# Second attention: GpSimd's sum ahead of its power, the next rows' load in slot 0, ScalarE's high half ahead of the norm

## The chip, the core and the metric

One core of a Trainium2 chip runs the whole program in one launch. The metric is the device time of one execution in microseconds. Of the kernel before three runs are given; their median is 3105.54 us.

## What is computed

Two layers, each an attention over a context and a mixture of eight experts, every one behind a layer norm and with its input added. The change lies in the second layer's attention. There x has 16 batches of 128 rows of 512 values, the context 128 further rows for each batch:

```python
q = (draft_hidden @ Wq.T).reshape(bsz, draft_len, H, HD)        # H = 16 heads of HD = 128
q = _rms_norm(q, q_norm_w).transpose(0, 2, 1, 3)
kv_in = jnp.concatenate([context_hidden, draft_hidden], axis=1) # 256 keys
k = (kv_in @ Wk.T).reshape(bsz, total_len, KVH, HD)             # KVH = 4
v = (kv_in @ Wv.T).reshape(bsz, total_len, KVH, HD).transpose(0, 2, 1, 3)
k = _rms_norm(k, k_norm_w).transpose(0, 2, 1, 3)
q = _rope(q, draft_position_ids)
k = _rope(k, full_position_ids)
scores = jnp.einsum('bhqd,bhkd->bhqk', q, k) * SCALE
probs = jax.nn.softmax(scores, axis=-1)
attn = jnp.einsum('bhqk,bhkd->bhqd', probs, v)
return attn.transpose(0, 2, 1, 3).reshape(bsz, draft_len, H * HD) @ Wo.T
```

## The kernel before

The program runs four parts in turn: first attention, first experts, second attention (`layer1_attention`), second experts. Precision close to float32 comes from splitting each operand into a high and a low float16 half; a product is three matmuls (high by high, high by low, low by high). So every value that goes into a product is made twice: ScalarE writes the high half (a copy to float16), VectorE subtracts it and writes the low half.

In the second attention a batch b has eight jobs, the projections `JOBS1` = KC, KD, Q0, VC, Q1, VD, Q2, Q3 (keys and values of context C and of x, D; four groups of four heads of queries), and four attention steps a = 0 to 3, one for each group of heads. Every engine has one queue, written by `run_pipeline` from a list of (kind, offset, stage). Time is counted in slots, eight to a batch. In each slot an engine goes through its list in the order written: a "job" stage with offset n runs job t - n, an "att" stage runs step a at slot `SCORE1[a]` + n, with `SCORE1` = 6, 8, 10, 12 (so a batch's attention runs beside the projections of the next one and the one after), an "in" stage with offset n runs in slot n for the batch after, an "end" stage n slots after the last score. The order inside a slot is the order of the list, and nothing is reordered at run time: what waits holds up all that stands behind it on its engine. The first two batches and the last two are written out, the rest is a loop.

The stages that the change and the prediction speak of, with the names of their tiles:

- SyncE's queue: `x_load` loads the next batch's x (`xt`, L1527) and context (`cx`, L1528), once the previous x is normed and the previous context split; `q_turn` (L1575) and `p_turn` (L1548) transpose by DMA the halves of the normed queries and keys and of the attention weights; `x_turn` (L1559) those of x.
- TensorE: `project` (12 matmuls of 512 columns into one of three banks `mm`), `scores` (`scb`, 12 matmuls of 256 columns), `pv` (attention output, `ovb`, 6 matmuls), `out_project` (`prb`, 12 matmuls). In even slots stand project, scores, out_project, in odd ones project, pv. `out_project(a)` stands one slot behind `pv(a)` and waits for `o_low(a)`.
- VectorE: `stats` reads a projection: four BN statistics (L1712) and the two products of the rotary embedding, `r1` and `r2` (L1717, L1720). `smax` (L1736) is the row maximum, `row_scale` (L1742, L1743) the reciprocal of the sums, `q_low` (L1731), `x_low` (L1692), `p_low` (L1750, four instructions) and `o_low` (L1758) the low halves.
- GpSimd: `scales` (L1988 to L1996) makes the RMS factors from the statistics, with a power (L1993, four values a row), and then the sum of the rotary products, `r1 + r2` (L1996, 128x512). `c_low` is the low half of the context, `tables` the sine and cosine tables.
- ScalarE: `c_high` (L1860) the high half of the context, `p_high` (L1907), `exps` (L1898) the exponentials with their row sums, `normalise` (L1878) the sum scaled by its RMS factor, in four instructions, `q_high` (L1889), `o_high` (L1914), `v_high` (L1867).

`o_high` is in the same odd slot as `exps` of two steps on, four slots behind the row maximum of its own step: in slot 3, for instance, ScalarE does the exponentials of step 2, norms Q0 and evicts the output of step 0.

Of the kernel before, what the change touches and what calls it, by code (L numbers as in the profile page):

```python
# [6 lines left out]
ALU = mybir.AluOpType  # L7
# [943 lines left out]
NN1, NV1, NA1 = len(NORM1), len(V1), 4  # L951
# [476 lines left out]
def layer1_attention(nc, I, x2_dram, x3_dram, w, wo, sincos, disp, expert_of_tile, row_of_tile, tile_oh):  # L1428


    with ExitStack() as ctx:
# [17 lines left out]
        r1 = s.sb("r1", [P, 2, 4, HD], F32)  # L1449
        r2 = s.sb("r2", [P, 2, 4, HD], F32)  # L1450
# [29 lines left out]
        rnb, rsum, rinv = (rc[:, n:n + 1] for n in range(3))  # L1480
# [25 lines left out]
        def at(k, per, b):  # L1506
            return b * per + (k + 1)

        def is0(b, k=0, below=1):

            return isinstance(b, int) and b == 0 and k < below
# [8 lines left out]
        def _(sp):  # L1520
# [40 lines left out]
            def q_turn(b, t, q):  # L1561
# [3 lines left out]
                for half, done in ((0, "qhi"), (1, "qlo")):  # L1565
# [5 lines left out]
                    if half == 0 and n >= 2 and not is0(b):  # L1571
# [2 lines left out]
                    out = kT[half][:, q, :, n, :] if n < 2 else qT[half][:, n - 2, :].rearrange("p (i t) -> p i t", t=P)  # L1574
                    sp.dma_start_transpose(out, nq[half][:, n % 2, :]).then_inc(q_turned[half][n % 2], 16)  # L1575

            run_pipeline(sp, [("in", 5, x_turn), ("job", 2, q_turn), ("att", 3, p_turn), ("end", 7, store), ("end", 2, residual), ("in", 1, x_load)],
                         NJ1, SCORE1, None, 2, HEAD1)
            sp.wait_ge(sem["out"], 16 * (B + 1))

# [259 lines left out]
        def _(act):  # L1840
# [29 lines left out]
            def normalise(b, t, q):  # L1870
                if t in v_no:
                    return
                job, n = norm_no[t], norm_no[t] % 2
                act.wait_ge(sem["rsum"], at(job, NN1, b))
                if not is0(b, job, 2):
                    act.wait_ge(sem["qlo"], at(job - 2, NN1, b))
                for i in range(4):
                    ins = act.activation(nrm[:, n, i * P:(i + 1) * P], r1[:, n, i, :], ACT.Copy,  # L1878
                                         scale=sc[:, n, 1, i:i + 1])
                ins.then_inc(sem["norm"], 1)  # L1880
# [51 lines left out]
            def r_gates(b, k, q):  # L1932
# [2 lines left out]
                act.activation(xr[:, q, DM + 1:RW], rex, ACT.Copy, scale=rinv).then_inc(sem["r_gate"], 1)  # L1935

            run_pipeline(act, [("in", 2, c_high), ("att", 2, p_high),
                               ("att", 1, exps), ("job", 1, normalise), ("job", 1, q_high),
                               ("att", 5, o_high), ("job", 1, v_high), ("in", 4, x_norm), ("in", 4, x_high),
                               ("end", 10, r_norm), ("end", 12, r_keep), ("end", 15, r_exp), ("end", 17, r_gates)],  # L1940
                         NJ1, SCORE1, None, 2, HEAD1)

# [1 line left out]
        def _(pool):  # L1944
# [33 lines left out]
            def scales(b, t, q):  # L1978
                if t in v_no:
                    return  # L1980
                job, n = norm_no[t], norm_no[t] % 2
                pool.wait_ge(sem["stat"], at(job, NN1, b))
                if not is0(b, job, 2):
                    pool.wait_ge(sem["norm"], at(job - 2, NN1, b))

                c = [sc[:, n, i, :] for i in range(2)]
                mean, spread = st[:, n, :, :, 1], st[:, n, :, :, 2]
                ch.link(pool.tensor_tensor(sq[:, n, :, :], mean, mean, ALU.mult))  # L1988
                ch.link(pool.tensor_scalar(sq[:, n, :, :], sq[:, n, :, :], HD / 2.0, None, ALU.mult))
                ch.link(pool.tensor_tensor(sq[:, n, :, :], sq[:, n, :, :], spread, ALU.add))  # L1990
                ch.link(pool.tensor_tensor(c[0], sq[:, n, :, 0], sq[:, n, :, 1], ALU.add))
                ch.link(pool.tensor_scalar(c[0], c[0], 1.0 / HD, 1e-6 * WS * WS, ALU.mult, ALU.add))
                pool.tensor_tensor(c[1], c[0], half[:, 0:4], ALU.pow).then_inc(sem["scal"], 1)  # L1993
                pool.wait_ge(sem["rot"], at(job, NN1, b))
                pool.wait_ge(sem["scal"], at(job, NN1, b))
                pool.tensor_tensor(r1[:, n, :, :], r1[:, n, :, :], r2[:, n, :, :], ALU.add).then_inc(sem["rsum"], 1)  # L1996

            def r_scale(b, k, q):
                pool.wait_ge(sem["r_stat"], b + 1)
# [366 lines left out]
```

## Time and profile before

| | |
|---|---|
| median of three runs | 3105.54 us (3100.19 to 3106.0) |
| the profiled execution, its own time | 3106.21 us |
| its span (first to last instruction) | 3104.4 us |
| mean granted TensorE clock | 0.970 |
| busy: TensorE, VectorE, ScalarE, GpSimd | 2848.2, 1829.6, 1703.5, 1741.2 us |
| second attention | about 2020 to 2812 us of the span |

The rows further down come from one profiled execution. A row of the waits says who waited for whom, in total, how often, and the longest. A row of the timeline has the start in microseconds from the span's start, the duration, the engine (SPq is SyncE's queue), the line, the operation and its output and input, and in square brackets how long the engine had idled before it and who ended that. Rows of one line are merged (x4). A matmul is pipelined: it is shown 0.38 us long, and the next begins before it ends.

### The profile page before, as it was taken

How to read it: one execution, taken by the hardware profiler on the slowest of the kernel's cores; microseconds unless marked ns; L12 is line 12 of the kernel's file. 1: busy time of each engine (PE TensorE's matmuls, PEld its weight loads, DVE VectorE, ACT ScalarE, POOL GpSimd, SP SyncE). 2: the span in 40 equal slices, each digit the busy share in tenths (PEclk: the TensorE clock that was granted, in tenths of full speed). 3: DMA queues.
4: the chain of work that ended last, by engine and by line, in shares of the span. 5: the costliest groups of instructions: out<-in, count | busy, mean ns of one | idle time of the engine just before them, and what ended most of it. 6: DMA issues, size and time to landing. Idle time of an engine off the chain costs nothing. (4 is left out here: it accounts for less than half of the span.)

```text
span 3104.4 us, 57661 instructions
## 1 busy us (share of the span) xinstructions
PE 2848.2 (92%) x16353; PEld 1637.9 (53%) x16354; DVE 1829.6 (59%) x5590; ACT 1703.5 (55%) x4562; POOL 1741.2 (56%) x2443
## 2 busy tenths in 40 slices
PE   4699999999999969999999999769999999985998
PEld 2366666666666635555555554335444444443665
DVE  4366666666666655444344344458888888863443
ACT  5578777877778732333233223346666666661332
POOL 6467777777777534554444455366666666631222
PEclk9799999999999989999999999889999999997999
DMA  6711121112111153554555456535555545657444
GB/s 241 251 42 56 51 86 48 48 55 79 58 48 55 54 200 120 161 157 125 147 159 151 137 141 186 141 80 113 122 113 123 122 112 122 123 106 286 80 83 70
DMA packets 467529, 360.89 MB, mean 116 GB/s; under 512 B 295520, under 2 KB 366304, under 8 KB 467424
## 3 DMA queue, kind: packets, MB, share of 16 engines
q1 hardware_dynamic: 404912, 282.85, 32.1%
q0 software_dynamic: 16496, 37.79, 6.3%
q10 hardware_dynamic: 46016, 38.99, 4.4%
q8 instruction: 49, 0.80, 0.1%
q14 instruction: 56, 0.46, 0.0%
HBM read 186.23 MB, written 110.39 MB: 96 GB/s over the span
## 5 line engine op out<-in xcount | busy, mean ns | idle before, releaser
L1393 POOL TENSOR_TENSOR e_st<-e_st,e_ws_tile 128x1024 f32<-128x1024 f32 x64 | 123.8, 1935 | 428.1 <-PE e_y L1149 417.2
L752 ACT ACTIVATE a_nrm<-a_mm,a_sc_t 128x128 f32<-128x128 f32 x768 | 290.8, 474 | 123.6 <-POOL a_sc_t L905 123.4
L603 DVE BATCH_NORM_STATS2 a_st<-a_mm 128x6 f32<-128x128 f32 x768 | 170.7, 285 | 289.5 <-PE a_mm L440 206.5
L439 PE MATMUL a_mm<-a_w_hi,a_xq_hi 128*128 128x512 f16 x768 | 296.6, 386 | 22.7 <-POOL a_xq_lo L887 15.7
L1187 ACT ACTIVATE e_hh<-e_ha 128x512 f16<-128x512 f32 x128 | 76.3, 596 | 411.7 <-PE e_ha L1134 410.1
L440 PE MATMUL a_mm<-a_w_hi,a_xq_lo 128*128 128x512 f16 x768 | 296.4, 386 | 0.0
L1282 DVE SCALAR_TENSOR_TENSOR e_hl<-e_ha,e_hh 128x512 f16<-128x512 f32 x128 | 88.4, 691 | 351.6 <-ACT e_hh L1187 351.2
L904 POOL TENSOR_TENSOR a_sc_t<-a_sc_t,a_mhalf 128x4 f32<-128x4 f32 x192 | 203.2, 1058 | 119.0 <-DVE a_sc_t L610 118.7
L1147 PE MATMUL e_y<-e_w2h,e_hh 128*128 128x512 f16 x640 | 242.6, 379 | 0.0
L1148 PE MATMUL e_y<-e_w2l,e_hh 128*128 128x512 f16 x640 | 242.6, 379 | 0.0
L1149 PE MATMUL e_y<-e_w2h,e_hl 128*128 128x512 f16 x640 | 242.6, 379 | 0.0
L1589 PE MATMUL a_mm<-l_wh,a_src_hi 128*128 128x512 f16 x512 | 196.2, 383 | 35.6 <-POOL a_src_lo L1963 27.5
L781 ACT ACTIVATE a_pr<-a_scb,a_nb 128x128 f32<-128x128 f32 x512 | 182.1, 383 | 71.2 <-DVE a_nb L615 54.5
L1132 PE MATMUL e_ha<-e_xeh,e_w1h 128*128 128x512 f16 x512 | 194.8, 380 | 4.2 <-DVE e_w1l L1274 4.2
L1590 PE MATMUL a_mm<-l_wl,a_src_hi 128*128 128x512 f16 x512 | 196.0, 383 | 0.0
L1591 PE MATMUL a_mm<-l_wh,a_src_lo 128*128 128x512 f16 x512 | 195.6, 382 | 0.0
L1133 PE MATMUL e_ha<-e_xel,e_w1h 128*128 128x512 f16 x512 | 194.8, 380 | 0.0
L1134 PE MATMUL e_ha<-e_xeh,e_w1l 128*128 128x512 f16 x512 | 194.7, 380 | 0.0
L1750 DVE SCALAR_TENSOR_TENSOR a_pql<-a_pr,a_ri,a_pqh 128x256 f16<-128x256 f32 x256 | 153.6, 658 | 1.8 <-ACT a_pqh L1907 1.8
L1898 ACT ACTIVATE a_pr<-a_scb,a_nb 128x256 f32<-128x256 f32 x256 | 117.3, 471 | 57.9 <-DVE a_nb L1736 57.7
L1907 ACT ACTIVATE a_pqh<-a_pr,a_ri 128x256 f16<-128x256 f32 x256 | 108.9, 496 | 70.8 <-DVE a_ri L1743 70.8
L461 PEld LDWEIGHTS a_scb<-a_kT,a_qT 128*128 128x128 f32 x1024 | 135.2, 193 | 22.7 <-issue 4.8
(366 smaller groups left out, 8246.6 us busy)
## 6 DMA issues: line engine op xcount, KB each, us to landing
e_st<-in_w SPq DMA_DIRECT2D x128, 512.0 KB, 4.2
disp<-a_empty SPq DMA_DIRECT2D x16, 2084.0 KB
e_st<-in_w1b SPq DMA_DIRECT2D x32, 352.0 KB, 3.1
disp<-a_empty SPq DMA_DIRECT2D x4, 2605.0 KB, 22.8
e_xb<-disp SPq DMA_DIRECT2D x40, 260.5 KB, 4.3
e_xb<-disp ACTq DMA_DIRECT2D x40, 260.5 KB
a_cx<-in_ctxT SPq DMA_DIRECT2D x32, 256.0 KB, 3.3
a_stage<-in_wprojT SPq DMA_DIRECT2D x16, 512.0 KB, 4.7
```

What stands on the lines that cost most here:

```text
L439: pe.matmul(out, xq_hi[:, n, c, :], w_hi[:, t, c, :], start=(c == 0), stop=False)
L440: mm = pe.matmul(out, xq_lo[:, n, c, :], w_hi[:, t, c, :], start=False, stop=(c == KT - 1))
L752: ins = act.activation(nrm[:, n % 2, i * P:(i + 1) * P], src[:, i * P:(i + 1) * P], ACT.Identity, bias=sc_t[:, n % 2, 3, i:i + 1], scale=s ...
L904: ch.link(pool.tensor_tensor(c[2], c[0], mhalf[:], ALU.pow))
L1132: pe.matmul(dst, wh, xh, start=(k == 0), stop=False)
L1133: pe.matmul(dst, wh, xl, start=False, stop=False)
L1147: pe.matmul(Y[i][:], hh, wh, start=(c == 0), stop=False)
L1148: pe.matmul(Y[i][:], hh, wl, start=False, stop=False)
L1149: mm = pe.matmul(Y[i][:], hl, wh, start=False, stop=(c == FC - 1))
L1589: pe.matmul(out, lhs[0], rhs[0], start=first, stop=False)
L1590: pe.matmul(out, lhs[0], rhs[1], start=False, stop=False)
L1591: return pe.matmul(out, lhs[1], rhs[0], start=False, stop=last)
```

## The change

Three edits to the second attention. Two move an entry within an engine's list: `x_load` on SyncE goes from the end of slot 1 to the front of slot 0, `o_high` on ScalarE from behind `normalise` and `q_high` to in front of them. The third swaps the last two instructions of `scales` on GpSimd: the sum of the rotary products comes before the power; the sum no longer waits for the power's semaphore `scal`, and `normalise` waits for it instead, beside `rsum`. No instruction on the data is added or removed. In the changed file the lines behind L1874 are one higher, and in `scales` the sum is L1995 and the power L1996.

```diff
--- before.py
+++ after.py
@@ -1574,7 +1574,7 @@
                     out = kT[half][:, q, :, n, :] if n < 2 else qT[half][:, n - 2, :].rearrange("p (i t) -> p i t", t=P)
                     sp.dma_start_transpose(out, nq[half][:, n % 2, :]).then_inc(q_turned[half][n % 2], 16)
 
-            run_pipeline(sp, [("in", 5, x_turn), ("job", 2, q_turn), ("att", 3, p_turn), ("end", 7, store), ("end", 2, residual), ("in", 1, x_load)],
+            run_pipeline(sp, [("in", 0, x_load), ("in", 5, x_turn), ("job", 2, q_turn), ("att", 3, p_turn), ("end", 7, store), ("end", 2, residual)],
                          NJ1, SCORE1, None, 2, HEAD1)
             sp.wait_ge(sem["out"], 16 * (B + 1))
 
@@ -1872,6 +1872,7 @@
                     return
                 job, n = norm_no[t], norm_no[t] % 2
                 act.wait_ge(sem["rsum"], at(job, NN1, b))
+                act.wait_ge(sem["scal"], at(job, NN1, b))
                 if not is0(b, job, 2):
                     act.wait_ge(sem["qlo"], at(job - 2, NN1, b))
                 for i in range(4):
@@ -1935,8 +1936,8 @@
                 act.activation(xr[:, q, DM + 1:RW], rex, ACT.Copy, scale=rinv).then_inc(sem["r_gate"], 1)
 
             run_pipeline(act, [("in", 2, c_high), ("att", 2, p_high),
-                               ("att", 1, exps), ("job", 1, normalise), ("job", 1, q_high),
-                               ("att", 5, o_high), ("job", 1, v_high), ("in", 4, x_norm), ("in", 4, x_high),
+                               ("att", 1, exps), ("att", 5, o_high), ("job", 1, normalise), ("job", 1, q_high),
+                               ("job", 1, v_high), ("in", 4, x_norm), ("in", 4, x_high),
                                ("end", 10, r_norm), ("end", 12, r_keep), ("end", 15, r_exp), ("end", 17, r_gates)],
                          NJ1, SCORE1, None, 2, HEAD1)
 
@@ -1990,10 +1991,9 @@
                 ch.link(pool.tensor_tensor(sq[:, n, :, :], sq[:, n, :, :], spread, ALU.add))
                 ch.link(pool.tensor_tensor(c[0], sq[:, n, :, 0], sq[:, n, :, 1], ALU.add))
                 ch.link(pool.tensor_scalar(c[0], c[0], 1.0 / HD, 1e-6 * WS * WS, ALU.mult, ALU.add))
+                pool.wait_ge(sem["rot"], at(job, NN1, b))
+                pool.tensor_tensor(r1[:, n, :, :], r1[:, n, :, :], r2[:, n, :, :], ALU.add).then_inc(sem["rsum"], 1)
                 pool.tensor_tensor(c[1], c[0], half[:, 0:4], ALU.pow).then_inc(sem["scal"], 1)
-                pool.wait_ge(sem["rot"], at(job, NN1, b))
-                pool.wait_ge(sem["scal"], at(job, NN1, b))
-                pool.tensor_tensor(r1[:, n, :, :], r1[:, n, :, :], r2[:, n, :, :], ALU.add).then_inc(sem["rsum"], 1)
 
             def r_scale(b, k, q):
                 pool.wait_ge(sem["r_stat"], b + 1)
```

TensorE's and VectorE's queues stay as they are. On ScalarE, slots 2 and 3 of a batch in the loop, before:

```order
L1860 ACTIVATE a_src_hi<-a_cx 128x512
L1907 ACTIVATE a_pqh<-a_pr,a_ri 128x2x128 x4
L1878 ACTIVATE a_nrm<-a_r,a_sc 128x128 x4
L1889 ACTIVATE a_nqh<-a_nrm 128x512
L1898 ACTIVATE a_pr,a_rs<-a_scb,a_nb 128x256 x4
L1878 ACTIVATE a_nrm<-a_r,a_sc 128x128 x4
L1889 ACTIVATE a_nqh<-a_nrm 128x512
L1914 ACTIVATE a_oh<-a_ovb 128x512
```

and now:

```order
L1860 ACTIVATE a_src_hi<-a_cx 128x512
L1908 ACTIVATE a_pqh<-a_pr,a_ri 128x2x128 x4
L1879 ACTIVATE a_nrm<-a_r,a_sc 128x128 x4
L1890 ACTIVATE a_nqh<-a_nrm 128x512
L1899 ACTIVATE a_pr,a_rs<-a_scb,a_nb 128x256 x4
L1915 ACTIVATE a_oh<-a_ovb 128x512
L1879 ACTIVATE a_nrm<-a_r,a_sc 128x128 x4
L1890 ACTIVATE a_nqh<-a_nrm 128x512
```

The high half of the attention output (`a_oh`) has moved in front of the norm and the high half of the query (`a_nqh`); the exponentials (`a_pr,a_rs`) stand where they stood. The same holds for each odd slot.

On SyncE's queue, from slot 7 to the first key transposes of slot 2, before:

```order
L1548 DMA_TRANSPOSE a_ph<-a_pqh 128x8x128
L1548 DMA_TRANSPOSE a_pl<-a_pql 128x8x128
L1575 DMA_TRANSPOSE a_qh<-a_nqh 128x4x128
L1575 DMA_TRANSPOSE a_ql<-a_nql 128x4x128
L1575 DMA_TRANSPOSE a_qh<-a_nqh 128x4x128
L1575 DMA_TRANSPOSE a_ql<-a_nql 128x4x128
L1548 DMA_TRANSPOSE a_ph<-a_pqh 128x8x128
L1548 DMA_TRANSPOSE a_pl<-a_pql 128x8x128
L1527 DMA a_xt<-x 128x512
L1528 DMA a_cx<-in_ctxT 128x4x128
L1575 DMA_TRANSPOSE a_kh<-a_nqh 128x4x128
L1575 DMA_TRANSPOSE a_kl<-a_nql 128x4x128
```

and now:

```order
L1548 DMA_TRANSPOSE a_ph<-a_pqh 128x8x128
L1548 DMA_TRANSPOSE a_pl<-a_pql 128x8x128
L1527 DMA a_xt<-x 128x512
L1528 DMA a_cx<-in_ctxT 128x4x128
L1575 DMA_TRANSPOSE a_qh<-a_nqh 128x4x128
L1575 DMA_TRANSPOSE a_ql<-a_nql 128x4x128
L1575 DMA_TRANSPOSE a_qh<-a_nqh 128x4x128
L1575 DMA_TRANSPOSE a_ql<-a_nql 128x4x128
L1548 DMA_TRANSPOSE a_ph<-a_pqh 128x8x128
L1548 DMA_TRANSPOSE a_pl<-a_pql 128x8x128
L1575 DMA_TRANSPOSE a_kh<-a_nqh 128x4x128
L1575 DMA_TRANSPOSE a_kl<-a_nql 128x4x128
```

The two loads have moved past three pairs of transposes, those of Q2, of Q3 and of the attention weights of step 0, and stand right behind the weights of step 3 (L1548).

On GpSimd the end of one `scales`, of Q0 in slot 2, before:

```order
L1963 TENSOR_TENSOR a_src_lo<-a_cx,a_src_hi 128x512
L1988 TENSOR_TENSOR a_sq<-a_st 128x8
L1989 TENSOR_SCALAR a_sq<-a_sq 128x8
L1990 TENSOR_TENSOR a_sq<-a_sq,a_st 128x8
L1991 TENSOR_TENSOR a_sc<-a_sq 128x4
L1992 TENSOR_SCALAR a_sc<-a_sc 128x4
L1993 TENSOR_TENSOR a_sc<-a_sc,a_half 128x4
L1996 TENSOR_TENSOR a_r<-a_r 128x512
```

and now:

```order
L1964 TENSOR_TENSOR a_src_lo<-a_cx,a_src_hi 128x512
L1989 TENSOR_TENSOR a_sq<-a_st 128x8
L1990 TENSOR_SCALAR a_sq<-a_sq 128x8
L1991 TENSOR_TENSOR a_sq<-a_sq,a_st 128x8
L1992 TENSOR_TENSOR a_sc<-a_sq 128x4
L1993 TENSOR_SCALAR a_sc<-a_sc 128x4
L1995 TENSOR_TENSOR a_r<-a_r 128x512
L1996 TENSOR_TENSOR a_sc<-a_sc,a_half 128x4
```

The sum (`a_r`) and the power (`a_sc<-a_sc,a_half`) have changed places.

## Rows read from the trace of the kernel before

**Rows 1.** Busy time by stage of the steady batches; per engine busy us (instructions), clock, DMA share, GB/s.
```profile
2211.90:2676.90 465.00, 431.57 (x2298) 222.25 (x2297) 403.35 (x971) 318.91 (x930) 306.22 (x610) 1.00 0.53 119
```

**Rows 2.** Waits of TensorE in the steady batches: us in total, times, longest us.
```profile
PE a_prb L1589 <- DVE a_ol L1758: 32.5, 20, 1.9
```

**Rows 3.** Timeline of TensorE, 2312 to 2337: start, us, engine, line [idle before].
```profile
2312.04 0.38 PE L1591 MATMUL a_ovb<-a_ph,a_vl 128*128 128x512 f16 x1
...
2318.62 0.38 PE L1589 MATMUL a_prb<-l_woh,a_oh 128*128 128x512 f16 x1 [1.91 <-DVE a_ol L1758]
...
2330.71 0.39 PE L1589 MATMUL a_prb<-l_woh,a_oh 128*128 128x512 f16 x1 [1.55 <-DVE a_ol L1758]
...
2336.98 0.38 PE L1591 MATMUL a_ovb<-a_ph,a_vl 128*128 128x512 f16 x1
```

**Rows 4.** Timeline of ScalarE, 2309 to 2338.
```profile
2309.30 0.63 ACT L1860 ACTIVATE a_src_hi<-a_cx 128x512 f16<-128x512 f32 x1 [5.32 <-DMA a_cx<-in_ctxT]
2309.84 1.69 ACT L1907 ACTIVATE a_pqh<-a_pr,a_ri 128x256 f16<-128x256 f32 x4
...
2313.26 0.46 ACT L1898 ACTIVATE a_pr<-a_scb,a_nb 128x256 f32<-128x256 f32 x1
...
2315.24 1.28 ACT L1878 ACTIVATE a_nrm<-a_r,a_sc 128x128 f32<-128x128 f32 x4
...
2317.17 0.58 ACT L1914 ACTIVATE a_oh<-a_ovb 128x512 f16<-128x512 f32 x1
...
2327.51 1.28 ACT L1878 ACTIVATE a_nrm<-a_r,a_sc 128x128 f32<-128x128 f32 x4
...
2329.35 0.58 ACT L1914 ACTIVATE a_oh<-a_ovb 128x512 f16<-128x512 f32 x1
...
2337.34 0.99 ACT L1878 ACTIVATE a_nrm<-a_r,a_sc 128x128 f32<-128x128 f32 x3
```

**Rows 5.** Timeline of SyncE's queue, 2291 to 2306.
```profile
2291.06 1.23 SPq L1548 DMA_TRANSPOSE a_pl<-a_pql  x1
...
2305.16 0.35 SPq L1527 DMA_DIRECT2D a_xt<-x  x1
```

**Rows 6.** Timeline of GpSimd, 2065 and 2304 to 2314.
```profile
2065.98 1.27 POOL L1996 TENSOR_TENSOR a_r<-a_r 128x512 f32<-128x512 f32 x1
...
2304.95 1.04 POOL L1993 TENSOR_TENSOR a_sc<-a_sc,a_half 128x4 f32<-128x4 f32 x1
2306.13 1.26 POOL L1996 TENSOR_TENSOR a_r<-a_r 128x512 f32<-128x512 f32 x1
...
2313.75 1.46 POOL L1996 TENSOR_TENSOR a_r<-a_r 128x512 f32<-128x512 f32 x1
```

**Rows 7.** Timeline of VectorE, 2066 and 2305 to 2327.
```profile
2066.14 1.67 DVE L1731 TENSOR_TENSOR a_nql<-a_nrm,a_nqh 128x512 f16<-128x512 f32 x1 [1.40 <-ACT a_nqh L1889]
...
2305.52 0.69 DVE L1731 TENSOR_TENSOR a_nql<-a_nrm,a_nqh 128x512 f16<-128x512 f32 x1
...
2310.41 1.22 DVE L1736 TENSOR_REDUCE a_nb<-a_scb 128x4 f32<-128x1024 f32 x1
...
2314.00 2.68 DVE L1750 SCALAR_TENSOR_TENSOR a_pql<-a_pr,a_ri,a_pqh 128x256 f16<-128x256 f32 x4
...
2326.56 1.66 DVE L1750 SCALAR_TENSOR_TENSOR a_pql<-a_pr,a_ri,a_pqh 128x256 f16<-128x256 f32 x4
```

**Rows 8.** Waits of VectorE in the steady batches.
```profile
DVE a_ol L1758 <- ACT a_oh L1914: 28.4, 20, 1.7
DVE a_nql L1731 <- ACT a_nqh L1889: 26.6, 20, 2.0
```

**Rows 9.** Waits of TensorE in the batches ahead of them, 2077.2 to 2211.9.
```profile
PE a_prb L1589 <- DVE a_ol L1758: 5.1, 5, 1.3
PE a_scb L1589 <- ACT a_pr L1898: 4.3, 1, 4.3
```

**Rows 10.** Waits of TensorE in the last full batch, 2676.9 to 2760.
```profile
PE a_prb L1589 <- DVE a_ol L1758: 4.9, 4, 1.7
```

## The prediction

> **What bounds the kernel now.** I first read the busy time by stage. Only the second attention is touched. Its ten steady batches, from one load of x to another, take 465.0 us, 46.5 each; TensorE is busy for 431.57 of them, VectorE for 403.35 (40.3 a batch), ScalarE for 318.91 and GpSimd for 306.22, at a granted clock of 1.00 [rows 1]. TensorE is thus the bound but for 33.4 us. Of these, 32.5 us are 20 waits in front of the output projection, for VectorE's low half of the attention output (`o_low`) [rows 2]. Two waits a batch, then; I followed both in the batch at 2300 to 2331 us.
>
> They stand at 2318.62 (1.91 us) and at 2330.71 (1.55 us). The product that the first needs began its last matmul at 2312.04, over six microseconds earlier [rows 3]. In between stands ScalarE: `o_high` starts only at 2317.17, since at 2309.30 ScalarE had idled 5.32 us for the context rows (`cx`), and from there it runs its queue without a gap: eviction of cx (`c_high`), `p_high`, two norms, the exponentials, `q_high`, and last `o_high`. In front of the second wait `o_high` stands at 2329.35 behind a norm of 1.28 us and `q_high`, though its product was ready [rows 4]. The load behind the 5.32 us was issued at 2305.16, behind four transposes of slot 1. It had landed at 2309.30, 4.1 us later. Nothing keeps it back but its place: the attention weights' last transpose of slot 7 was issued at 2291.06 [rows 5].
>
> **The load in slot 0.** No transfer is added. The pair is issued right behind the transpose at 2291.06, so at about 2292.3, some 13 us earlier, and lands near 2296. ScalarE reaches `c_high` at 2304, so the 5.32 us go. The two issues (0.35 us for the first) now stand in front of Q2's transposes in SyncE's queue and delay the first of them by up to 0.8 us; its reader, the scores two slots on, comes some ten microseconds later, so this is hidden. Without that cover it would cost 0.8 us a batch. The semaphores it waits for belong to the previous x and cx, long consumed.
>
> **ScalarE's high half before the norm.** The same instructions. `o_high` now follows the exponentials directly: at 2329.35 it would have stood at 2327.51, 1.84 us earlier [rows 4], more than the 1.55 us wait it feeds. It waits for the product, and the norm, `q_high`, VectorE's `q_low` and a transpose are queued behind it. At the first place the product was done at 2312.4 and the exponentials at 2315.2; the tightest place is slot 7, where the product's last matmul ends at 2337.36 and the norm behind the exponentials starts at 2337.34 [rows 3, 4]. So the added wait costs nothing; its price where it does is the last rival. The norm and `q_high` come 0.5 us later than before against the exponentials, which `q_low` meets: between `o_high` and `q_high` lie 1.28 + 0.53 us, while VectorE has `o_low` and the row scales to do, 1.0 us. So up to 0.8 us of a new wait in each of four slots.
>
> **GpSimd's sum before its power.** The wait for the power's own semaphore goes, 0.14 us a job: the power at 2304.95 lasts 1.04 us and the sum starts at 2306.13 [rows 6]. The norm needs both, so it gains 0.14 us and no more. But the sum starts 1.18 us earlier, and that matters to VectorE. Four `p_low` took 2.68 us at 2314.00, beside a sum of GpSimd from 2313.75 to 2315.21, and 1.66 us at 2326.56, without one; a `q_low` took 1.67 us beside the sum at 2065.98 and 0.69 us at 2305.52, inside a power [rows 6, 7]. A sum thus holds up VectorE's operations on two SBUF operands until it ends; a power does not. Three of four `p_low` a batch pay about 1.0 us each. With the sum earlier it lies mostly beside the score maximum, which reads PSUM (1.22 us at 2310.41). In two slots, of KD and of Q3 or KC, it meets `q_low` instead, by some 0.65 us. Net for VectorE: 1 to 2 us a batch less, between 0 and 3. The Trainium skill, "SBUF — State Buffer", section "Who interferes with whom", says that a VectorE instruction with two SBUF inputs and a GpSimd instruction that reads SBUF shut each other out for the whole instruction. For the sum the trace agrees; for the power it does not, as the 0.69 us show. By the rule the power would stand where the sum stood and the swap would gain VectorE nothing: third rival.
>
> **Walked through the batch.** Both engines behind the first wait start from the same state at 2303.4. cx is evicted at once, `p_high` waits for the row scales and ends at 2307.2, the norm of KD at 2308.6. VectorE's final sum and maximum end at 2311.6 as before, but now ScalarE is free: exponentials to 2313.5, `o_high` to 2314.0, `o_low` (behind `q_low` and `p_low`, which start at 2311.6 and take 0.6 + 1.66 us) to 2314.9. TensorE is through with the scores at 2316.5, so the 1.91 us go, with a slack of 1.6 us. What follows is 2.1 us earlier on TensorE and 2.9 us on VectorE, which waits less for ScalarE there. Second place: TensorE is ready at 2329.16 less 2.1, 2327.0; the exponentials end at 2327.5 less 2.9, 2324.6, `o_high` at 2325.2, `o_low` at 2325.8: slack 1.2 us. At the two places without a wait today the order of events stays and the slack, under 1 us, is the smallest. VectorE needs 40.3 us of the new 43.15 and may wait 2.8 of today's 5.5 us a batch [rows 1, 8]; its waits for `o_high` (28.4 us in ten batches) nearly go, those for `q_high` (26.6) stay at 1 to 3 us a batch, and the ports give back 1 to 2.
>
> **The sum**, against the profiled execution (3106.21 us, span 3104.4). Steady batches: all 33.4 us of idle time go in the walk. A wait also costs the refill of the array behind it, an estimated 0.17 us in each of 20 (of a matmul's 0.38 us [rows 3] about half otherwise lies under the next one), so up to 37; with 1 us of new waits in three of four batches 26. I take 34. The batches ahead of them, 2077 to 2212: 5.1 us for `o_low` and 4.3 for the exponentials [rows 9], the latter behind a ScalarE that had waited for cx too; of 9.4 I take 8 (4 to 9.4). The wait for the transposed weights (2.0) stays. The last full batch, to 2760: 4.9 [rows 10], I take 4 (2 to 4.9); after 2760 no projections are left to cover and nothing changes. In all 46 us: 3060.2 for this execution. The median of the runs, 3105.54, stands 0.7 lower: 3059.5. Bounds: 51 us (3054) and 32 us (3074).
>
> **The rivals.**
> 1. *VectorE becomes the bound.* It is at 87% now and would be at 93%. If `q_high` is late in all four odd slots (3.2 us) and a wait of 1 us at KD or Q3 stays, a batch takes 40.3 + 4.2 = 44.5 us. Then 20 us of the steady part and 6.5 of the rest go: 3079. For it: under 1 us of slack at two places. Against it: the earlier sum and the gap-free stretches on VectorE that the walk shows. Chance 0.13.
> 2. *Nothing measurable.* The 5.32 us on ScalarE are replaced by its wait for the row scales, `o_high` comes as late as before: 3105, also if the order did not change at run time. Against it: the exponentials at 2313.26 follow the 5.32 us through an unbroken queue. Chance 0.04.
> 3. *The power blocks like the sum.* `p_low` is held up three times as before and `q_low` by 0.65 us twice more: VectorE 40.3 + 1.3, with waits of 2.2 us 43.8 a batch. 27 + 8 + 4 = 39 us: 3066.5. Against it is the `q_low` inside a power. The page of the skill speaks for it. Chance 0.12.
> 4. *Slower.* `o_high` waits for TensorE's product while norms are ready behind it. If the product were late at all four places, `q_low` would wait for the norm and `q_high` (1.8 us) four times a batch, 7.2 in place of the 2.84 us for `o_high`, on top of the 2.66 for `q_high`: 40.3 + 7.2 + 2.7 = 50.2 us a batch, 3.7 more than now, over thirteen batches 48 us: 3154. It decides once VectorE's waits pass 6.2 us a batch (46.5 less 40.3). Against it: the product ends no later than the exponentials in every odd slot. Chance 0.04.
>
> **How the numbers follow.** Forecast case 0.67, at 3059.5 (its own range 3053 to 3067). With rivals 3 (3066.5) and 1 (3079) the range 3052 to 3079 holds over 8 in 10. 0.2% is 6.2 us, about what a measurement can tell from no change. Forecast and rivals 1 and 3 are faster by more: 0.92. Within it: 0.04. Slower: 0.04.
>
> **What would show it.** Right: TensorE's waits for `o_low` between two loads near zero, a batch of 43 us, VectorE above 90% busy there; ScalarE's wait for cx gone; `p_low` nearly always 1.66 us for four, a few `q_low` over 1 us; the power without effect on either. Wrong: a batch over 44 us with TensorE still waiting for `o_low`, VectorE without gaps (rival 1), long waits of `o_high` for the product (rival 4), or `p_low` of 2.6 us beside a power (rival 3). If the cx wait is gone and the batch is still 46.5 us, the reading of the chain was wrong.

## The result, and the profile after

| | before | after |
|---|---|---|
| median of 4 runs (us) | 3104.72 (3100.19 to 3106.0) | 3047.6 (3043.18 to 3051.39) |
| profiled execution, span | 3106.21, 3104.4 | 3051.39, 3049.6 |
| granted clock over the span | 0.970 | 0.973 |

The ratio is 0.9818, with a 95% interval of [0.9801, 0.9835]: the change takes 57 us off. The forecast was 3059.5 with a range from 3052 to 3079, so the direction and the order of size are right and the measured time lies 4.4 us below the range's low end. The interval stands for 3042.9 to 3053.5 us, so the range's low end lies inside it; the forecast itself is 12 us off.

The span is 54.8 us shorter. To find where, both traces are cut at the same matmuls: each kernel has 3664 of them in this part, up to the last output projection, in the same order. The pieces are the prediction's own, that is the batches ahead, the ten steady ones, the last full one, and the rest. The last row of each view holds nine batches and is cut at the stores of x3 on SyncE's queue (L1540). (The kernel writes out the first four batches and the last two, since `HEAD1` counts pairs; its loop holds the ten between them.) The view is the windows view of either kernel; its columns are those of [rows 1]. Before:

```profile
2026.34:2211.94 185.60, 164.10 (x824) 81.72 (x825) 145.93 (x330) 117.30 (x332) 119.05 (x247) 0.95 0.49 99
2211.94:2676.98 465.04, 431.61 (x2298) 222.29 (x2296) 403.39 (x971) 318.91 (x930) 306.26 (x610) 1.00 0.53 119
2676.98:2761.89 84.91, 77.84 (x417) 39.93 (x414) 69.20 (x175) 57.99 (x170) 51.05 (x100) 1.00 0.59 115
2761.89:2795.07 33.18, 26.67 (x129) 14.12 (x130) 17.57 (x56) 15.92 (x50) 3.62 (x8) 0.90 0.50 104
2225.90:2644.30 418.40, 388.72 (x2072) 200.48 (x2070) 363.74 (x874) 287.02 (x837) 276.02 (x549) 1.00 0.53 119
```

After:

```profile
2027.92:2201.00 173.08, 161.63 (x824) 81.42 (x825) 143.16 (x334) 118.72 (x335) 122.14 (x248) 0.97 0.54 110
2201.00:2628.50 427.50, 427.50 (x2299) 224.99 (x2296) 384.42 (x969) 318.70 (x930) 311.68 (x611) 1.00 0.58 129
2628.50:2707.43 78.93, 76.96 (x417) 40.39 (x414) 68.26 (x172) 57.02 (x169) 50.26 (x98) 1.00 0.55 114
2707.43:2740.82 33.39, 26.88 (x129) 13.94 (x130) 17.55 (x56) 15.92 (x50) 3.62 (x8) 0.90 0.45 103
2211.30:2596.40 385.10, 385.10 (x2072) 202.82 (x2071) 346.27 (x874) 287.14 (x838) 280.96 (x549) 1.00 0.58 129
```

The second column is the piece's length, the third TensorE's busy time. The gain is 12.5 + 37.5 + 6.0 - 0.2 = 55.8 us; 0.6 more behind the last of these matmuls and 1.6 less in front of the first make the 54.8. In the nine batches the two columns are now equal: TensorE is busy for all of the 385.10 us, 42.79 a batch (46.49 before). They lost 29.7 us of idle time, and 3.6 us of busy time on top (388.72 to 385.10, for the same 2072 matmuls). Spread over the 21 waits that went, that is 0.17 us each, which fits the prediction's estimate of a refill.

A cut at the stores is good for a period and less so for a sum: a store of x3 stood 11.0 us behind its batch's last output projection before (batch 2) and stands 7.4 us behind it now, so such a cut would count 3.7 us too many for the first batches.

The waits of the other engines in the loop after, most first (us in total, times, longest):

```profile
ACT a_pr L1899 <- DVE a_nb L1736: 57.4, 27, 2.7
...
DVE a_nql L1731 <- ACT a_nqh L1890: 23.6, 27, 1.3
ACT a_oh L1915 <- PE a_ovb L1591: 17.1, 18, 1.0
...
DVE a_ol L1758 <- ACT a_oh L1915: 5.4, 18, 0.3
```

ScalarE's wait for `cx` (5.32 us in [rows 4]) is gone from the list, VectorE's for `o_high` fell from 28.4 us in ten batches [rows 8] to 5.4 in nine, that for `q_high` hardly moved (26.6 in ten, 23.6 in nine). A new one stands there: in two of the four odd slots of a batch `o_high` waits for TensorE's product, 0.95 us at a time. One such place, and VectorE behind it, in the timelines of ScalarE, VectorE and GpSimd after:

```profile
2313.59 0.21 ACT L1899 ACTIVATION_READ_ACCUMULATOR a_pr<-a_scb,a_nb 128x1 f32 x1
2314.72 0.60 ACT L1915 ACTIVATE a_oh<-a_ovb 128x512 f16<-128x512 f32 x1 [0.91 <-PE a_ovb L1591]
2315.21 1.26 ACT L1879 ACTIVATE a_nrm<-a_r,a_sc 128x128 f32<-128x128 f32 x4
2316.59 0.63 ACT L1890 ACTIVATE a_nqh<-a_nrm 128x512 f16<-128x512 f32 x1
```

```profile
2315.42 0.68 DVE L1758 SCALAR_TENSOR_TENSOR a_ol<-a_ovb,a_oh 128x512 f16<-128x512 f32 x1
...
2317.35 0.69 DVE L1731 TENSOR_TENSOR a_nql<-a_nrm,a_nqh 128x512 f16<-128x512 f32 x1 [0.96 <-ACT a_nqh L1890]
...
2322.22 1.19 DVE L1731 TENSOR_TENSOR a_nql<-a_nrm,a_nqh 128x512 f16<-128x512 f32 x1 [1.07 <-ACT a_nqh L1890]
2323.34 1.66 DVE L1750 SCALAR_TENSOR_TENSOR a_pql<-a_pr,a_ri,a_pqh 128x256 f16<-128x256 f32 x4
...
2327.71 0.92 DVE L1743 TENSOR_SCALAR a_ri<-a_ri 128x4 f32<-128x4 f32 x1
2328.54 0.68 DVE L1731 TENSOR_TENSOR a_nql<-a_nrm,a_nqh 128x512 f16<-128x512 f32 x1
```

```profile
2321.60 1.27 POOL L1995 TENSOR_TENSOR a_r<-a_r 128x512 f32<-128x512 f32 x1
...
2322.83 1.48 POOL L1996 TENSOR_TENSOR a_sc<-a_sc,a_half 128x4 f32<-128x4 f32 x1
...
2327.33 1.27 POOL L1995 TENSOR_TENSOR a_r<-a_r 128x512 f32<-128x512 f32 x1
2328.57 1.55 POOL L1996 TENSOR_TENSOR a_sc<-a_sc,a_half 128x4 f32<-128x4 f32 x1
```

`o_high` comes 0.9 us after the exponentials, still in time for TensorE; the norm, `q_high` and `q_low` pay for it. The four `p_low` took 1.66 us.

The first batches have a different cause beside the waits. TensorE between 2070 and 2100, before and then after (the granted clock is the third number from the end):

```profile
2070.00:2080.00 10.00, 6.02 (x35) 2.98 (x33) 9.96 (x22) 3.71 (x13) 6.16 (x10) 1.00 0.75 115
2080.00:2090.00 10.00, 5.74 (x27) 2.86 (x25) 3.60 (x7) 8.23 (x24) 4.63 (x8) 0.88 0.46 87
2090.00:2100.00 10.00, 9.40 (x45) 4.28 (x45) 9.64 (x19) 7.54 (x21) 7.79 (x16) 0.95 0.53 112
```

```profile
2070.00:2080.00 10.00, 8.37 (x45) 4.07 (x43) 9.87 (x23) 7.92 (x24) 7.84 (x12) 1.00 0.59 119
2080.00:2090.00 10.00, 8.63 (x47) 4.20 (x45) 8.52 (x19) 8.53 (x23) 6.73 (x18) 1.00 0.56 107
2090.00:2100.00 10.00, 10.00 (x54) 5.15 (x53) 9.62 (x20) 6.71 (x21) 7.63 (x15) 1.00 0.52 107
```

Before, TensorE idles for 8.2 us of the 20 from 2070 to 2090 and runs part of the time up to 2100 at the lower of its two levels (1.2 in place of 2.4 GHz); after, it idles for 3.0 us and the clock stays up.

### The profile page after: what moved, and what is told of

Same layout as the page of the kernel before. It is cut to its first block and busy times, and to the rows that moved or that the text cites. A ratio compares the mean times of both kernels' runs of the same rounds, so it can differ in the third digit from the quotient of the medians.

```text
span 3049.6 us, 57678 instructions
## 1 busy us (share of the span) xinstructions
PE 2834.9 (93%) x16353; PEld 1636.1 (54%) x16354; DVE 1807.4 (59%) x5590; ACT 1703.4 (56%) x4562; POOL 1749.1 (57%) x2443
## 5 line engine op out<-in xcount | busy, mean ns | idle before, releaser
L1879 ACT ACTIVATE a_nrm<-a_r,a_sc 128x128 f32<-128x128 f32 x384 | 122.1, 395 | 39.0 <-POOL a_sc L1996 25.8
L1395 POOL TENSOR_TENSOR e_w2l<-e_st,e_w2h 128x1024 f16<-128x1024 f32 x64 | 139.1, 2173 | 5.1
```

## The experiments

They answer three questions: which part of the change carries the gain, whether VectorE has any slack left, and what was missed in the forecast. For the time of a batch each profile is cut at the same stores; the median of the kernel before on the same chip was between 3101.9 and 3103.7 us in all of them.

### One part at a time

The load alone (SyncE's list as in the change, the rest as before):

```
-run_pipeline(sp, [("in", 5, x_turn), ("job", 2, q_turn), ..., ("end", 2, residual), ("in", 1, x_load)],
+run_pipeline(sp, [("in", 0, x_load), ("in", 5, x_turn), ("job", 2, q_turn), ..., ("end", 2, residual)],
```

> The load in slot 0 alone. Theory (two waits with two causes): ScalarE's wait for cx goes and with it the first of the two waits a batch (1.9 us) and most of the exponentials' wait near 2087 us; the second (1.55 us) stays, since o_high still stands behind a norm and q_high. About 25 us less: 3080. Rival (one chain, everything late because of cx): both waits go, 3050 to 3060. Rival (the load is covered otherwise): 3105.

3083.19 us, ratio 0.9938 [0.9923, 0.9953], 20.5 us off. A batch takes 45.13 us; TensorE still waits for `o_low`.

`o_high` alone:

```
-("att", 1, exps), ("job", 1, normalise), ("job", 1, q_high), ("att", 5, o_high), ("job", 1, v_high),
+("att", 1, exps), ("att", 5, o_high), ("job", 1, normalise), ("job", 1, q_high), ("job", 1, v_high),
```

> ScalarE's high half in front of the norm, alone. Theory: o_high comes 1.8 us earlier at both places. The second wait goes; the first only in part, since o_low then stands behind p_low on VectorE (end at 2316.7, TensorE ready at 2316.6), so 0.7 of 1.9 us stay. ScalarE's wait for cx stays at about 5 us a batch. About 28 us less: 3077. Rival (the product is late, norms pile up behind o_high): 3105 or more.

3073.24 us, 0.9908 [0.9892, 0.9923], 30.5 us off, 44.41 us a batch. This part is the larger one, though ScalarE's wait for `cx` is still there. Both times lie within 4 us of what was expected. The waits in the loop, of the load alone and then of `o_high` alone:

```profile
PE a_prb L1589 <- DVE a_ol L1758: 18.0, 18, 1.5
```

```profile
ACT a_src_hi L1860 <- DMA a_cx<-in_ctxT: 43.5, 9, 5.3
PE a_prb L1589 <- DVE a_ol L1758: 7.3, 12, 0.7
PE a_scb L1589 <- ACT a_pr L1898: 1.6, 5, 0.6
```

The load removes one wait a batch nearly whole and leaves the other. `o_high` at its new place shortens both, because it comes one norm and one `q_high` earlier each time.

In the first batches neither part does much alone. The expectation that the load would take most of the exponentials' wait near 2087 us was wrong: that wait fell from 4.26 to 1.87 us, but TensorE then waited 3.33 us for `o_low` at 2087.50. With `o_high` alone the two were 2.68 and 0.63 us; with both parts, 0.73 and 0.63.

The swap alone:

```
-pool.tensor_tensor(c[1], c[0], half[:, 0:4], ALU.pow).then_inc(sem["scal"], 1)
 pool.wait_ge(sem["rot"], at(job, NN1, b))
-pool.wait_ge(sem["scal"], at(job, NN1, b))
 pool.tensor_tensor(r1[:, n, :, :], r1[:, n, :, :], r2[:, n, :, :], ALU.add).then_inc(sem["rsum"], 1)
+pool.tensor_tensor(c[1], c[0], half[:, 0:4], ALU.pow).then_inc(sem["scal"], 1)
```

> GpSimd's sum in front of its power, alone. Theory (a sum holds up VectorE's operations on two SBUF operands, a power does not): p_low takes 1.66 us for four nearly everywhere in place of 2.68, VectorE is busy 1 to 2 us less a batch, but waits for ScalarE instead; time 3095 to 3105. Rival (the power blocks as well): p_low stays at about 2.6 us in three of four steps, 3104 to 3106.

3106.08 us over ten runs, 1.0007 [0.9998, 1.0017]: no gain. That is a microsecond above the theory's range, where the rival had it, but for the reason the theory names. VectorE did get its time back. Its `p_low` in and around the loop, before and with the swap alone (ns, least, median, most):

```profile
L1750 DVE SCALAR_TENSOR_TENSOR a_pql<-a_pr,a_ri,a_pqh x144: 470/473/1526, 2233.5 to 2641.6; 128x256 f16<-128x256 f32 x144
```

```profile
L1750 DVE SCALAR_TENSOR_TENSOR a_pql<-a_pr,a_ri,a_pqh x145: 469/472/476, 2219.7 to 2639.9; 128x256 f16<-128x256 f32 x145
```

No `p_low` is held up any more, and no power holds one up. VectorE is busy for 350.11 of 420.3 us in nine batches instead of 363.74 of 418.4, and waits for `o_high` instead (45.1 us, against 28.4 in ten batches before). In the profile before, three `p_low` a batch had taken 1.4 to 1.5 us in place of 0.47. The saved 1.5 us a batch were in front of a wait.

Load and `o_high` without the swap:

> The load and the high half, without the swap. Theory (TensorE bounds, VectorE has room): p_low is held up by the sum as before, VectorE is busy over 90%, and still a batch takes 42.8 to 43.2 us: 3048 to 3054. Rival (the swap is what frees VectorE, which would otherwise bound): waits for o_low remain, a batch takes 43.8 us or more, 3060 to 3070.

3052.5 us, 0.9834 [0.9821, 0.9848]: 51.2 us off, the sum of the two alone (51.0). A batch takes 42.88 us between the stores. Between its own matmuls TensorE needs 385.14 us for nine batches, 42.79 each, and that is what the whole change needs too, to the hundredth (2205.09 to 2590.23 us without the swap, 2204.03 to 2589.17 with it). So the theory holds: in the loop the swap adds nothing to the other two.

### The parts in pairs, and the whole once more

> The whole change once more, on the same chip as the runs beside it. Theory A (the load and o_high carry the change, the swap is worth nothing since VectorE has slack): 3048 to 3054 us, like the load and o_high without the swap (3052.5). Theory B (the swap is worth 1 to 2 us a batch of VectorE time once TensorE no longer waits): 10 us or more below 3052.5, so under 3043 us.

> The load in slot 0 and the swap, o_high behind the norm as before. Theory A: 3083 to 3086 us, as the load alone (3083.2), with some 1.5 to 2 us a batch of TensorE's waits for o_low left. Theory B: the swap frees VectorE, o_low comes earlier and the time falls under 3078 us.

> o_high in front of the norm and the swap, the load behind the transposes as before. Theory A: 3072 to 3077 us, as o_high alone (3073.2). Theory B: under 3068 us, since what waits are left there (a_prb 7.3 us, a_scb 1.6 us in nine batches) are VectorE's.

The whole gave 3047.91 us, 0.9821 [0.9807, 0.9834], and 42.79 us a batch again: theory A. Load and swap: 3082.56, 0.9935 [0.992, 0.995], as the load alone. `o_high` and swap: 3066.97, 0.9888 [0.9871, 0.9904], 43.61 us a batch against 44.41 for `o_high` alone. That is under theory B's 3068, not in theory A's 3072 to 3077: with the wait for `cx` still there and `o_high` early, the swap is worth 0.8 us a batch. TensorE's waits for `o_low`, 7.3 us with `o_high` alone, are gone there, so VectorE was the late one.

### Has VectorE slack?

`o_low` issued twice in front of each output projection, the rest as in the change:

```
+ch.link(dve.scalar_tensor_tensor(out=oT[1][:, a % 2, :], in0=OVB[:], scalar=1.0 / PS,
+                                 in1=oT[0][:, a % 2, :], op0=ALU.mult, op1=ALU.subtract))
 dve.scalar_tensor_tensor(out=oT[1][:, a % 2, :], ...).then_inc(sem["olo"], 1)
```

> The change with VectorE's o_low issued twice in front of each output projection: 4 times some 0.4 us (an eviction of 512 columns from PSUM) more on VectorE a batch and as much later for TensorE. Theory A (TensorE is 100% busy and o_low has 1 us or more of slack at each place): 3048 to 3056 us, 42.8 us a batch, TensorE without waits, VectorE at 93 to 94%. Rival (VectorE at 90% is itself the second chain and has no slack left): 1 to 1.6 us a batch more, 3060 to 3068 us, with TensorE waiting for a_ol.

3086.43 us, 0.9947 [0.9932, 0.9963]: 38.5 us more than the change, more than either theory allowed. A copy takes 0.69 us, not the 0.4 expected, 2.8 us a batch; but in the loop most of the loss is something else. VectorE's timeline in that kernel:

```profile
2368.77 0.69 DVE L1760 SCALAR_TENSOR_TENSOR a_ol<-a_ovb,a_oh 128x512 f16<-128x512 f32 x1
2374.90 0.18 DVE L1742 RECIPROCAL a_ri<-a_rs 128x4 f32<-128x4 f32 x1 [5.45 <-issue]
```

Its exponentials had ended at 2366.7. Four times in the loop, once in two batches, VectorE stands still for 5 us in front of an instruction whose inputs are ready. The DMA view has 76 transfers of instructions on one queue where the change has 57:

```profile
q14 instruction: 76, 0.62, 0.1%
```

So the next kernel adds the eight instructions to the loop but hardly any work: the copy of `o_low` covers one column.

> The change with a one-column copy of o_low in front of each o_low: eight instructions more in VectorE's loop of two batches, some 0.1 to 0.2 us each, so 0.3 to 0.8 us of work a batch. Theory C (the 38 us of the doubled o_low came from the number of instructions in VectorE's loop: idle times of 5 us for nothing the profile shows once in two batches, and 76 instruction transfers in place of 56): 3075 to 3090 us, the same 5 us idle times, 70 or more instruction transfers. Rival (they came from the 0.7 us that each copy takes): 3046 to 3056 us and 56 instruction transfers.

3057.26 us, 0.986 [0.9844, 0.9875], again 76 transfers and four idle times of up to 4.8 us. Theory C holds in its mechanism and not in its price: it said 3075 us or more, and the loss is 9.7 us, since TensorE's queue covers most of each idle time (16.8 us of them cost nine batches 6.4 us). The rival's 0.7 us a copy is a part of the doubled `o_low`'s loss: its batches with a standstill take 48.2 to 48.8 us, those without one 44.03 to 44.11, 1.24 us more at the least than the change, for 2.8 us of copies.

A longer instruction in place of an added one: the reciprocal in the row scales (L1742) over a wider source (the lines show 512 columns).

```
-ch.link(dve.reciprocal(ri[:, a % 2, :], rs[:]))
-dve.tensor_scalar(ri[:, a % 2, :], ri[:, a % 2, :], PS, None, ALU.mult).then_inc(sem["rinv"], 1)
+ch.link(dve.reciprocal(rw[:], rs[:].unsqueeze(1).to_broadcast([P, 128, 4])))
+dve.tensor_scalar(ri[:, a % 2, :], rw[:, 0, :], PS, None, ALU.mult).then_inc(sem["rinv"], 1)
```

> The change, with VectorE's reciprocal in the row scales running over 512 columns (the four sums read 128 times, into a spare tile) in place of 4: the same number of instructions, some 0.5 us more of VectorE four times a batch, 2.1 us a batch. Theory A (TensorE bounds, VectorE has slack at every place): 3045 to 3055 us, TensorE still without waits, VectorE at 94 to 95%. Rival (VectorE's chain is as long as TensorE's and each 0.5 us shows): up to 2.1 us a batch, 3065 to 3078 us, TensorE waiting for a_ol or a_pr.

3187.67 us, 1.0279 [1.0263, 1.0295]. The dose was wrong: 512 columns took 3.34 us, against 0.17 for 4. VectorE then bounds the loop, 455.79 us busy of 467.8 (97%), 51.98 us a batch. Two smaller doses, 80 and 128 columns:

> The change with the reciprocal over 80 columns in place of 4. The run over 512 columns showed 3.34 us against 0.167, 6.2 ns a column, so some 0.47 us more of VectorE four times a batch, 1.9 us a batch. Theory A (o_low has slack of 1 us or so at every place): 42.8 us a batch, 3045 to 3055 us, TensorE's waits under 1 us a batch. Theory D (TensorE and the chain through VectorE and ScalarE are equally long): 1 to 1.9 us a batch more, 3060 to 3075 us, TensorE waiting for a_pr.

> The same over 128 columns: 0.77 us more four times a batch, 3.1 us a batch, so 41.4 us of work for VectorE. Theory A: VectorE's 3.7 us of waits a batch are used up first; with the 1.3 us of waits that stay when VectorE bounds (the run over 512 columns) 42.7 to 43.2 us a batch, 3048 to 3060 us. Theory D: 2 to 3.1 us a batch more, 3075 to 3090 us.

3049.0 us, 0.9824 [0.9809, 0.9839], and 3066.36 us, 0.9886 [0.987, 0.9901]. The loops, over 80 and then over 128 columns:

```profile
2211.40:2596.90 385.50, 385.50 (x2074) 203.01 (x2072) 356.13 (x872) 287.03 (x837) 277.17 (x547) 1.00 0.62 129
```

```profile
2209.90:2607.30 397.40, 388.99 (x2075) 201.24 (x2074) 372.21 (x873) 285.97 (x838) 273.87 (x549) 1.00 0.57 125
```

A reciprocal of 0.63 us four times a batch (1.9 us more) is hidden whole: 42.83 us a batch, TensorE without a gap; VectorE's wait for `q_high` shrank from 23.6 to 16.5 us. One of 0.93 us (3.1 us more) adds 1.37 us, and TensorE waits for the exponentials (7.9 us in 12 waits). The path from the row scales over the score maximum and the exponentials to TensorE thus has between 0.47 and 0.77 us of slack a slot. That is within the "under 1 us" that the walk gave for the two places without a wait. TensorE never waits for `o_low` in either run, so the 1.6 and 1.2 us that the walk gave in front of `o_low` were not tested.

### Has TensorE's work the last word?

The output projection without its product of the high half of the attention output and the low half of the weights; that part is missing from the output.

```
-mm = products(PRB[:], [...o for o in oT], [...x for x in wo], a == 0 and i == 0, a == NA1 - 1 and i == 3)
+pe.matmul(PRB[:], o[0], x[0], start=a == 0 and i == 0, stop=False)
+mm = pe.matmul(PRB[:], o[1], x[0], start=False, stop=z)
```

> The change with the output projection's third product left out (high half of the attention output by the low half of the weights, so the output lacks that part): 16 matmuls fewer on TensorE a batch, 16 times 0.21 us = 3.4 us. Theory A (TensorE alone bounds the batch and VectorE follows at 38.4 us of work and 3.7 us of waits): the gain is cut off where VectorE's chain begins, a batch of 40.5 to 42 us, 3020 to 3038 us, TensorE waiting for a_ol or a_pr. If VectorE's chain is no shorter than TensorE's: 42.8 us a batch, 3045 us or more.

3038.89 us, 0.9799 [0.9784, 0.9814]. The batch is 42.60 us, 0.2 shorter, with 3.4 us of matmuls gone. The loop's waits of TensorE and VectorE:

```profile
DVE a_nql L1732 <- ACT a_nqh L1891: 27.1, 27, 2.4
...
PE a_scb L1589 <- ACT a_pr L1900: 14.2, 18, 1.1
...
PE a_rb L1656 <- ACT a_xrT L1927: 9.1, 9, 1.1
```

So neither theory is right as put: TensorE has no gap in the change, and yet a second limit stands 0.2 us under it. It is no engine's work, for VectorE is busy for 345.13 of these 383.4 us and ScalarE for 286.00. It looks like a ring of waits, which takes hold from batch to batch: the second and third batches still take 39.3 and 41.3 us, and only from there on 42.6. (That is also where most of the 9 us of time come from.) TensorE waits for the exponentials and, once a batch, for the router's transposed rows (`a_rb`), `q_low` for `q_high`. That the ring passes through the norm and `q_high` fits the hidden 1.9 us of the reciprocal, which lies in front of `q_low`'s wait; it was not tried by itself.

### The last step of a batch, later

Behind the loop the change leaves TensorE waiting for the exponentials, 2.6 us and 0.9 us, since VectorE's last step of a batch, `final`, stands in front of the score maximum of its slot:

```
-run_pipeline(dve, [("end", 7, final), ("att", 2, row_scale), ("att", 1, smax), ("job", 2, q_low), ...
+run_pipeline(dve, [("att", 2, row_scale), ("att", 1, smax), ("end", 7, final), ("job", 2, q_low), ...
```

> The change with VectorE's last step of a batch (the sum of projection and residual) behind the score maximum of its slot in place of in front of it. In the loop nothing changes (TensorE never waits there): 42.8 us a batch. Behind the loop TensorE waits 2.6 us and 0.9 us for the exponentials behind that step, and these should go: 3044 to 3047 us where the change gives 3048. If the maximum itself then comes no earlier, 3048; if the later x3 delays the router's chain, some us more.

> The load in slot 0, o_high in front of the norm, the last step of a batch on VectorE behind the score maximum, and GpSimd's power in front of its sum as before. If the swap is worth nothing: 3038 to 3043 us, as with the swap (3039.9). If it is worth the 0.3 us a batch by which VectorE is busier without it: 3043 to 3048 us, with TensorE waiting for a_ol or a_pr in the loop.

3039.89 us, 0.9804 [0.9791, 0.9818], 4 us under what was expected; without the swap 3047.63, 0.9825 [0.9812, 0.9838]. The second time is in the range in which the swap is worth something, but the waits in the loop that were to come with it are not there: both take 385.14 us for nine batches. The gain over the change looks like 8 us, but the touched part of the profile, first load to last store, is only 2.9 us shorter (717.8 against 720.7). The rest is where the second attention starts: 2016.6 here, 2015.3 to 2024.2 over all runs. The three versions side by side on one chip:

> The change itself, beside the next two on one chip: 3047 to 3049 us, 42.8 us a batch, 718 to 721 us from the first load of x to the last store.

> The load and o_high without the swap. If the swap is worth the 0.1 us a batch of the profiles, 1 to 2 us more than the change; if the medians so far (3052.5 against 3047.9) are right, 4 to 6 us more.

> The change with the last step of a batch behind the score maximum. If it is worth what the waits behind the loop show, 1 to 3 us less than the change and 716 to 718 us from the first load to the last store; if the medians so far (3039.9 against 3047.9) are right, 6 to 9 us less.

The change 3047.46 (0.9819 [0.9805, 0.9832]), without the swap 3050.06 (0.9834 [0.982, 0.9847]), with `final` later 3044.9 (0.9815 [0.9802, 0.9829]). The intervals overlap, so neither step can be told from nothing by its time. The profiles have `final` later 3.3 and 2.7 us shorter behind the loop, in the two pairs. TensorE's waits behind the loop, side by side, in the change and with `final` later:

```profile
PE a_scb L1589 <- ACT a_pr L1899: 3.5, 2, 2.6
PE a_prb L1589 <- DVE a_ol L1758: 3.0, 3, 1.4
```

```profile
PE a_prb L1589 <- DVE a_ol L1758: 3.6, 3, 2.0
...
PE a_scb L1589 <- ACT a_pr L1899: 0.9, 1, 0.9
```

The wait of 2.6 us is gone, 0.6 us of it comes back at `o_low`. This comes from VectorE's order behind the loop; the loop itself stays at 42.79 us.

## Why the prediction was right and where it was wrong

**The mechanism is the one forecast.** Both waits a batch for `o_low` went, the load and `o_high` each took a part, the wait for `cx` went, and TensorE waits for no transpose in the loop. "A batch of 43 us" was 42.79.

**The step that failed is the sum: it priced TensorE's shorter busy time, the refills and the clock, at almost nothing.** It read "In all 46 us"; the span gave 54.8. The idle time that it counted was 33.4 + 9.4 + 4.9 = 47.7 us, and 48.6 went. But the same matmuls also took 7.3 us less of busy time, for which the sum had a term in the steady batches alone, and its "I take" gave that away again. By its three terms:

| | taken (upper end) | measured | of it idle | of it busy |
|---|---|---|---|---|
| ten steady batches | 34 (37) | 37.5 | 33.4 | 4.1 |
| batches ahead | 8 (9.4) | 12.5 | 10.0 | 2.5 |
| last full batch | 4 (4.9) | 6.0 | 5.1 | 0.9 |
| behind it | 0 | -0.2 | 0 | -0.2 |

- *"I take 34" for the ten steady batches.* All 33.4 us of idle time went, as the walk had it, and 0.2 us of busy time with each of 20 waits, where the estimate was 0.17. The 3 us taken off for "1 us of new waits in three of four batches" should have stayed: no new wait came.
- *"The last full batch, to 2760: 4.9, I take 4."* Its four waits went whole, and their refills with them.
- *"Of 9.4 I take 8" for the batches ahead.* The waits that it counted gave 8.0 us (4.44 for `o_low`, 3.53 for the exponentials). What it left out is the rest. The wait for the exponentials at 2073 fell from 1.95 to 0.97 us and was not counted; the one for the transposed weights fell from 2.03 to 0.65 ("The wait for the transposed weights (2.0) stays" was wrong); 0.3 us more of idle time stand before 2070. And the busy time, 2.5 us, had no term at all: 1.3 us of it went between the matmuls at 2080.20 and 2100.08, where the clock rose from 0.85 and 0.98 to 1.00, 0.5 before 2070, where it rose from 0.85 to 0.89, and 0.7 behind 2100, four waits at 0.17 us, at 1.00 in both.

In the three stretches of 10 us above, the granted clock rose from 1.00, 0.88, 0.95 to 1.00 three times. The profiles tie it to the gaps, though not in every execution: of the six profiles without one of the two parts none has 1.00 in all three stretches (the load alone 1.00, 0.88, 0.95; `o_high` alone 0.83, 1.00, 1.00), of the fourteen with both twelve have, and the other two show 0.83, 1.00, 1.00. That the gaps caused it is argued from this and was not tried apart.

So 8.8 us are missing in the sum: 3.5 + 4.5 + 2.0, less 0.2 behind the last full batch and 1.0 outside these matmuls, where the second attention started 1.6 us later, which the change does not touch. The other 3.1 us between 3059.5 and 3047.6 are spread between executions: the profiled one, 3051.39, was the slowest of the four and stands 3.8 us above their median, where the one before stood 0.7 above.

**The walk-through had one fact wrong that cost nothing.** "The product ends no later than the exponentials in every odd slot" does not hold once the exponentials come earlier. The walk's own numbers said so: TensorE 2.1 us earlier, VectorE and the exponentials 2.9, and at the tightest place both had ended together. `o_high` waits for the product in two of four slots, 0.95 us each. That is the last rival's mechanism. It stays harmless: the slack of about 0.5 us a slot was measured with this wait in place, and VectorE's waits stay far from the 6.2 us a batch from which that rival decides: 4.3 (385.10 less 346.27, over nine).

**The rivals.** *VectorE becomes the bound* did not happen: 90% busy, and 1.9 us a batch more are hidden. It is near: 3.1 us more show. *Nothing measurable* fell with the first result. *The power blocks like the sum* fell with the swap alone: `p_low` never over 476 ns, and 1.66 us for four at 2323.34, beside a power that ran from 2322.83 to 2324.31. The Trainium skill, "SBUF — State Buffer", section "Who interferes with whom", which speaks for this rival, is right here for the sum; for the power it is not, as far as VectorE is held up (the other direction stands in the last section). But the sum's move was worth something in VectorE's load alone: with the other two parts in place it took its work from 39.7 to 38.5 us a batch, 1.5 us alone, within the forecast's 1 to 2 (0 to 3), and nothing off the loop's time. The gain of the change is thus the load's 20.5 and `o_high`'s 30.5 us, and at most a few us of the swap, outside the loop.

**What stays open.** Which steps close the ring that stands at 42.6 us; and what sets the clock's dips in the first batches, which two profiles with both parts still show.

## What to carry to other kernels

When a wait on the bounding engine is found, follow the late operand back through the queue of each engine on its way, and ask at each for the first item that is not needed for it: here a load behind four transposes and a norm ahead of an eviction, worth 51 us with no work removed. Price a wait that goes by its length and the refill behind it, in every stretch and not only in the steady one, and where the engine starts up look whether the work behind its gaps runs at the lower clock. Where a walk shows no new wait take the whole wait and its refill, with the smaller value as the range's end. Once the bounding engine has no gap, take some work off it before trusting that it alone bounds: here a ring of waits stood 0.2 us under it.

## What the runs showed of the hardware

- Eight more instructions in VectorE's loop of two batches cost 9.7 us even when they do next to nothing: up to 4.8 us of standstill once in two batches, and 76 instruction transfers for 57. The Trainium skill, "Runtime: NRT & Kernel Launch", section "Instruction fetch mechanics", says that a taken branch to code outside the instruction memory's window forces a fetch before execution goes on; the loop's standstills and transfers agree with that, and that the fetch is the cause was not shown apart.
- VectorE's reciprocal costs 0.17, 0.63, 0.93 and 3.34 us over 4, 80, 128 and 512 columns, 6.2 ns a column, where `o_low` takes 0.68 us for its 512 columns from PSUM.
- GpSimd's sum also holds up a VectorE operation with a single SBUF operand: the row scales' second step (L1743), 128x4, took 0.92 us at 2327.71, beside a sum, where it takes 0.17 without one (median 0.33, most 0.93 in the loop after; at most 0.19 in the loop of the load and `o_high` with the power first). `q_low` goes from 0.68 to 1.2 us in the same way.
- The other way round a `q_low` lengthens GpSimd's power: 1.48 and 1.55 us at 2322.83 and 2328.57, against 1.04. At 2311.55 the power came first, 0.08 us ahead of four `p_low`, and neither was lengthened (1.04 and 1.65 us).
